# Attention row maxima from four part products in two row tiles, and the last four batches' layer-norm work moved from GpSimd to VectorE

## The chip, the cores and the metric

One core of a Trainium2 chip runs the whole program in one launch. The metric is the device time of that launch in microseconds, the median of several runs; lower is better. The core has five engines with a queue of instructions each: TensorE (PE in the profile, its weight loads PEld), VectorE (DVE), ScalarE (ACT), GpSimd (POOL) and SyncE (SP), which here only issues DMAs. Engines wait for each other through semaphores; a wait blocks everything that stands behind it on its engine.

## What is computed

Two layers of an adaptive-layer-norm network on 32 batches of 256 tokens with 128 features. The change lies in the first half of layer 0, attention with 16 heads of 8 features, followed by the second layer norm and the choice of two of eight experts for each token:

```
h   = layernorm(x) * (1 + scale_a[b]) + shift_a[b]
q,k = rope(h), rope(h @ w_k)              # 16 heads of 8 features, 256 tokens
p   = softmax(q @ k.T / sqrt(8))          # per head, 256 x 256
x   = x + gate_a[b] * ((p @ v) @ w_o + b_o)
h2  = layernorm(x) * (1 + scale_b[b]) + shift_b[b]
two of eight experts for each row of h2, by top-2 of h2 @ gate_w
```

A softmax does not change when a number is taken off all scores of a row, so the row maximum that the kernel subtracts has only to be near the true one.

## The kernel before

The program has stages: set-up, attention with the routing in front of the experts (the function `attention`), the experts of layer 0, and then layer 1, which is the longer part of the time. Only `attention` is touched.

**The loop.** Each engine has its own program, written out for every turn `i`; nothing but the written order and the semaphores decides what runs when. A turn handles several batches at different lags: batch `i` is normed, projected and roped; batch `i - 1` is stored and reloaded; `i - 2` (MAX) gets its row maxima; `i - 3` and `i - 4` their scores, exponentials and values; `i - 5` (OUT) the output projection; `i - 6` (LAST) the residual. Then come the second norm and the routing, for pairs of batches (`plan.groups`). There are 41 turns (0 to 40); `plan.var_at`, `root_at`, `norm_at`, `first_at`, `rank_at`, `quick_at` and `scattered_by` say in which turn a pair has its variance, root, modulation, choice, ranking and scatters. In the middle of the stage turns alternate: in even ones a pair is chosen (`top_of`, `first_of_top`, `first_chosen`, `second_chosen`), in odd ones it is ranked (`places`, `distances`, `slot_rows`, `limits`, `weights`).

**Three parts.** Each float32 of q and k is split into three bfloat16 parts. All nine products of parts are summed by one contraction over 9 x 8 = 72 rows (KROWS); `Q9` and `K9` hold these 72 rows, with two more for the row maximum, which the score product subtracts. SP stores the parts to DRAM (L512) and loads them back nine times over in eight DMAs for each batch (L525, L526, L528).

**Slots.** A turn on TensorE has eight slots (L1081): the maximum product of head 2p (L1012, two matmuls), four score matmuls (L1025), the maximum product of head 2p + 1, and values (L1039). Projections, transposes and logits stand between the slots. The scores of this batch's maximum are written to `MX`, a PSUM tile with two halves, head `h` to half `h % 2`. VectorE takes each head's maximum over the keys (`row_max`, L798) and so frees the half. The product of head h waits for the maximum of head h - 2. Between the maxima VectorE has its other steps: the bias (L921), the split of the maxima (L928, L930), rope (L955), the division by the sums (L977, L979), the statistics (L299) and the routing.

**The tail.** After the last maximum (turn 33) GpSimd does the residual (L609, L613), the variance (L554 to L560), the offset (L565), the modulation (L575, L581) and the scatters of rows to the experts' slots (L593), in this order on one queue. Each scatter is an indirect DMA of one tile of 128 rows; 128 are needed. When all places are known, SP writes eight blocks of padding rows (L541). Only then does the next stage start.

## Time and profile before

| | us |
|---|---|
| median of 3 runs | 3188.53 |
| lowest, highest | 3188.18, 3190.11 |
| profiled execution | 3185.01 |
| its span, first to last instruction | 3183.2 |

The profile's first part gives the busy time of each engine over the span: PE 2733.4 us (86%), DVE 2515.7 (79%), ACT 2236.9 (70%), POOL 2259.3 (71%). Its second part divides the span into 40 slices; the attention stage is in the first nine. The mean granted TensorE clock is 0.934 of full speed (2.4 GHz), and 0.5 stands for 1.2 GHz. The costliest group of this stage is the row maximum L798, 337.5 us in 512 instructions.

### The profile page before, as it was taken

The page shows a single profiled execution, that of the slowest core. Times are in us where ns is not written, and L with a number is a line of the kernel's source. Part 1 is how long each engine was busy: PE and PEld are TensorE (multiplying, and loading weights), DVE is VectorE, ACT ScalarE, POOL GpSimd, SP SyncE. Part 2 cuts the span into 40 slices and gives each one's busy share as a digit, 9 for nine tenths or more (in the row PEclk, how much of TensorE's full clock was granted, in tenths as well). Part 3 has the DMA queues.
Part 4 walks back from the last instruction along what each step waited for, and adds up shares of the span by engine and source line. Part 5 has one row for each costly group of instructions (what it writes and reads, how often), then busy time and mean ns, then how long its engine had stood idle before and what let it go on. Part 6 is the DMA issues. An engine that isn't in the chain of part 4 may idle for free. (4 is left out here: it accounts for less than half of the span.)

```text
span 3183.2 us, 56565 instructions
## 1 busy us (share of the span) xinstructions
PE 2733.4 (86%) x18747; PEld 2079.7 (65%) x18747; DVE 2515.7 (79%) x3550; ACT 2236.9 (70%) x4091; POOL 2259.3 (71%) x1731
## 2 busy tenths in 40 slices
PE   5999999829999977888888989888998888779984
PEld 3555555418999834666666666666766666679983
DVE  5788888723444446999999999999999999967993
ACT  2677777612222249999999999999999998656651
POOL 3356667552333348999999999999999999733664
PEclk6999999959999988999999999999999999889995
DMA  6555656316666662222222222222222222322231
GB/s 140 106 107 117 117 113 119 78 47 194 197 190 195 164 218 81 81 75 71 85 80 82 82 74 79 81 81 84 75 72 86 80 82 80 93 56 82 74 87 39
DMA packets 209174, 321.85 MB, mean 101 GB/s; under 512 B 37786, under 2 KB 118070, under 8 KB 204282
## 3 DMA queue, kind: packets, MB, share of 16 engines
q1 hardware_dynamic: 195666, 299.13, 34.9%
q0 software_dynamic: 12224, 18.42, 1.9%
q8 instruction: 161, 2.64, 0.4%
q14 instruction: 115, 0.94, 0.1%
q10 hardware_dynamic: 1008, 0.72, 0.1%
HBM read 269.92 MB, written 55.84 MB: 102 GB/s over the span
## 5 line engine op out<-in xcount | busy, mean ns | idle before, releaser
L1824 POOL TENSOR_TENSOR resid_x<-s_ux,s_B_rows 128x1024 f32<-128x1024 f32 x256 | 605.3, 2365 | 83.7 <-PE s_y L2554 82.7
L2385 DVE TENSOR_TENSOR_SCAN resid_x<-s_dA,resid_x 128x1024 f32<-128x1024 f32 x256 | 582.3, 2275 | 28.8 <-ACT s_dA L2036 23.2
L2393 DVE TENSOR_TENSOR_SCAN resid_x<-s_late,s_back_in 128x1024 f32<-128x1024 f32 x256 | 583.9, 2281 | 20.2 <-ACT s_late L2046 17.1
L2554 PE MATMUL s_y<-identity,resid_x 128*128 128x128 f32 x4096 | 558.7, 282 | 9.6 <-issue 8.8
L2554 PEld LDWEIGHTS s_y<-identity,resid_x 128*128 128x128 f32 x4096 | 498.6, 146 | 65.1 <-issue 40.6
L1832 POOL TENSOR_TENSOR resid_x<-resid_x,s_C_rows 128x1024 f32<-128x1024 f32 x192 | 454.0, 2365 | 0.9 <-DVE resid_x L2385 0.9
L798 DVE TENSOR_REDUCE a_row_max<-a_maxscores 128x2 f32<-128x512 f32 x512 | 337.5, 683 | 67.9 <-PE a_maxscores L1012 62.3
L2400 DVE TENSOR_TENSOR resid_x<-resid_x,s_C 128x1024 f32<-128x1024 f32 x320 | 382.7, 1196 | 6.0 <-PE s_C L2529 6.0
L2541 PE MATMUL s_back_in<-identity,resid_x 128*128 128x128 f32 x2048 | 292.3, 289 | 98.9 <-ACT resid_x L2057 52.6
L2036 ACT ACTIVATE s_dA<-s_dt,s_A 128x510 f32<-128x510 f32 x512 | 330.0, 676 | 66.2 <-DVE resid_x L2385 65.1
L2046 ACT ACTIVATE s_late<-s_dt,s_A 128x510 f32<-128x510 f32 x512 | 338.0, 710 | 0.0
L2541 PEld LDWEIGHTS s_back_in<-identity,resid_x 128*128 128x128 f32 x2048 | 239.8, 148 | 141.6 <-issue 81.9
L1324 POOL DMA_INDIRECT choice_outputs<-e_y,e_idx x142 | 137.8, 970 | 272.8 <-DVE e_y L1315 248.9
L668 ACT ACTIVATE a_probs<-a_scores 128x1024 f32<-128x1024 f32 x256 | 261.4, 1024 | 98.7 <-PE a_scores L1025 88.8
L1296 DVE TENSOR_TENSOR e_g<-e_silu,e_ps 128x512 f32<-128x512 f32 x142 | 97.7, 688 | 253.1 <-PE e_ps L1266 233.3
L1285 ACT ACTIVATE e_silu<-e_ps 128x512 f32<-128x512 f32 x142 | 84.8, 597 | 242.1 <-PE e_ps L1262 238.7
L3112 PE MATMUL k_psY<-k_coef_T,k_basis 128*128 128x128 f32 x2048 | 235.6, 277 | 7.1 <-ACT k_basis L3075 4.3
L3112 PEld LDWEIGHTS k_psY<-k_coef_T,k_basis 128*128 128x128 f32 x2048 | 232.9, 194 | 7.9 <-DVE k_basis L3003 4.7
L1012 PE MATMUL a_maxscores<-a_K,a_Q 72*128 72x256 bf16 x1024 | 203.9, 283 | 29.7 <-DVE a_row_max L798 17.1
L2581 PE MATMUL s_prep<-s_xT,k_coef_T 128*128 128x512 f32 x464 | 210.9, 596 | 2.7 <-ACT s_xT L2134 1.6
L2529 PE MATMUL s_C<-s_bc_parts,s_w_sel 96*128 96x512 bf16 x320 | 126.7, 396 | 87.1 <-DVE resid_x L2400 87.1
L2057 ACT ACTIVATE resid_x<-s_uT,s_bT 128x256 f32<-128x256 f32 x432 | 185.2, 498 | 0.8
(461 smaller groups left out, 5696.3 us busy)
## 6 DMA issues: line engine op xcount, KB each, us to landing
s_B_rows<-forward_rows SPq DMA_DIRECT2D x256, 256.0 KB, 3.3
e_w<-L_ffn_w_by_expert SPq DMA_DIRECT2D x71, 768.0 KB, 4.5
s_C_rows<-forward_rows SPq DMA_DIRECT2D x192, 256.0 KB, 3.3
a_Q<-split_qk SPq DMA_DIRECT2D x96, 192.0 KB
split_qk<-a_parts SPq DMA_DIRECT2D x32, 384.0 KB
e_x<-slot_inputs SPq DMA_DIRECT2D x71, 132.0 KB
a_K<-split_qk SPq DMA_DIRECT2D x64, 128.0 KB
s_late<-choice_outputs SPq DMA_DIRECT2D x16, 512.0 KB, 5.0
```

The source lines that it names most:

```text
L668: nc.scalar.activation(PT[:, q % 4].rearrange("p a b t -> p (a b t)"), ST[:, q % 2].rearrange("p a b t -> p (a b t)"), ACT.Exp, scale=SCAL ...
L798: nc.vector.tensor_reduce(mx[b % 2][:, h, :], MX[:, h % 2], AX.X, ALU.max).then_inc(S["max_done"], 1)
L1824: tt(R[s, 0], ux[par][:], brow[s % BRING][:].unsqueeze(1).broadcast_to([P, C2, W]), ALU.mult).then_inc(S["in_ready"], 1)
L1832: tt(r, r, crow[k % CRING][:].unsqueeze(1).broadcast_to([P, C2, W]), ALU.mult).then_inc(S["part_pool"], 1)
L2036: last = func(dA[:, c2, :, 1:T], dt[par][:, 0, c2, :].rearrange("p (g t) -> p g t", t=T)[:, :, 1:T], ACT.Exp, scale=Wt["A"][:, 0, c2, s:s ...
L2046: last = func(dec[s % 2][:, c2, :, 0:T - 1], dt[par][:, 1, c2, :].rearrange("p (g t) -> p g t", t=T)[:, :, 0:T - 1], ACT.Exp, scale=Wt["A" ...
L2385: nc.vector.tensor_tensor_scan(r, a, r, 0.0, ALU.mult, ALU.add).then_inc(S["scanned"], 1)
L2393: nc.vector.tensor_tensor_scan(r[:, ::-1], a[:, ::-1], b[:, ::-1], 0.0, ALU.mult, ALU.add).then_inc(S["scanned"], 1)
L2400: tt(r, r, CP[:].unsqueeze(1).broadcast_to([P, C2, W]), ALU.mult).then_inc(S["part_dve"], 1)
L2541: last = nc.tensor.transpose(bP[:, c2, k // TC, (k % TC) * P:(k % TC + 1) * P], bt[s % 2][:, k, c2 * P:(c2 + 1) * P], core.ident[:])
L2554: last = mm(YP[:, t, c2 * P:(c2 + 1) * P], R[s, d][:, c2, t * P:(t + 1) * P], core.ident[:], is_transpose=True, start=((s, d) == (0, 1) an ...
L3112: last = mm(psY[:, j % 2, k * D:(k + 1) * D], basis[j % 2][:, m, k * P:(k + 1) * P], WT[:, m, :], start=(m == EARLY[0] and k == 0), stop=( ...
```

## The change

Two parts, and a third that follows from the second.

- **Row maxima.** The product for the maximum no longer contracts all 72 rows, but 32 (`LEAD`): the four products of the first two parts. The order of the nine blocks in `Q9` and `K9` becomes different for heads 0 to 7 and for heads 8 to 15 (`Q_RUNS`, `K_RUNS`), so that these four stand in rows 0 to 31 for the first eight heads and in rows 32 to 63 for the last eight. A slot takes heads p and p + 8 together, one into each half of `MX`, with one semaphore step for the pair, and waits for both maxima of the pair before. The score product still contracts all 72 rows and the two of the maximum, so only the number that is subtracted changes a little. The reload takes 22 DMAs for each batch, each for eight heads.
- **The last four batches** (28 to 31). VectorE does their residual, variance, offset and modulation, in its own order.
- **Scatters** from turn 34 on are asked for as soon as their group is ranked, in eights.

```
+LEAD = 4 * DH
+Q_RUNS = (((0, 0, 2), (2, 0, 2), (4, 0, 3), (7, 2, 1), (8, 2, 1)), ((0, 0, 3), (3, 2, 1), (4, 0, 2), (6, 0, 3)))
+K_RUNS = (((0, 0, 2), (2, 1, 1), (3, 0, 1), (4, 2, 1), (5, 2, 1), (6, 0, 3)), ((0, 2, 1), (1, 2, 1), (2, 0, 2), (4, 0, 2), (6, 1, 1), (7, 0, 1), (8, 2, 1)))
...
-            sent = min(open_rows, sent + (4 if i <= B else 6)) if i < B + last else open_rows
+            sent = min(open_rows, sent + (4 if i <= B else 6)) if i < B + 2 else open_rows
...
-    LOADS = 3 * PARTS - 1
+    LOADS = sum(len(runs) for runs in (*Q_RUNS, *K_RUNS))
...
+    OWN_TAIL = B - 4
...
+                        for tile, w, runs in ((Q9[n], 0, Q_RUNS), (K9[n], 1, K_RUNS)):
+                            for half in range(2):
+                                for block, part, count in runs[half]:
+                                    sp.dma_start(tile[block * DH:(block + count) * DH, half * PAIRS:(half + 1) * PAIRS, :].rearrange("p h t -> p (h t)"),
+                                                 rows[w, part * DH:(part + count) * DH, half * PAIRS * T:(half + 1) * PAIRS * T]).then_inc(loaded[n], 16)
...
                 def row_max(i, h):
                     if live(i, MAX):
                         b = i - MAX
-                        dve.wait_ge(S["max_ps"], H * b + h + 1)
+                        dve.wait_ge(S["max_ps"], PAIRS * b + h // 2 + 1)
                         if h == 0:
                             at(dve, S["maxT_ps"], b - 1)
-                        nc.vector.tensor_reduce(mx[b % 2][:, h, :], MX[:, h % 2], AX.X, ALU.max).then_inc(S["max_done"], 1)
+                        nc.vector.tensor_reduce(mx[b % 2][:, h // 2 + PAIRS * (h % 2), :], MX[:, h % 2], AX.X, ALU.max).then_inc(S["max_done"], 1)
...
+                        if b >= OWN_TAIL:
+                            x_add(dve, nc.vector, b)
+                            new_stats(b)
+                    if i in plan.var_at and 2 * plan.var_at[i] >= OWN_TAIL:
+                        variance(dve, nc.vector, chain, plan.var_at[i])
+                    if i in plan.root_at and 2 * plan.root_at[i] >= OWN_TAIL:
+                        offset(dve, nc.vector, plan.root_at[i])
+                    if plan.early(i) is not None and plan.early(i) >= OWN_TAIL:
+                        modulate(dve, nc.vector, plan.early(i))
+                        modulate(dve, nc.vector, plan.late(i))
...
-                def max_scores(i, h):
+                def max_scores(i, p):
...
-                        at(pe, S["max_done"], H * b + h - 1)
+                        at(pe, S["max_done"], H * b + 2 * p)
                         for k in range(TC):
-                            last = mm(MX[:, h % 2, k, :], Q9[n][0:KROWS, h, k * P:(k + 1) * P], K9[n][0:KROWS, h, :], start=True, stop=True)
+                            for half in range(2):
+                                lead, h = slice(half * LEAD, (half + 1) * LEAD), p + PAIRS * half
+                                last = mm(MX[:, half, k, :], Q9[n][lead, h, k * P:(k + 1) * P], K9[n][lead, h, :], start=True, stop=True)
                         last.then_inc(S["max_ps"], 1)
...
                 def slot(i, p):
-                    max_scores(i, 2 * p)
+                    max_scores(i, p)
                     scores(i, p)
-                    max_scores(i, 2 * p + 1)
                     values(i, p)
```

Where it stands in the order: TensorE, two slots in the middle of the stage, before the change (`a_maxscores` is `MX`, `a_K` and `a_Q` the loaded parts, `a_out` the weighted values).

```order
L1124 MATMUL a_proj<-a_qk,a_rot 128x512
L1012 MATMUL a_maxscores<-a_K_0,a_Q_0 128x256 x2
L1025 MATMUL a_scores<-a_Q_2,a_K_2 128x256 x4
L1012 MATMUL a_maxscores<-a_K_0,a_Q_0 128x256 x2
L1039 MATMUL a_out<-a_probs,a_V 32x256 x4
L1012 MATMUL a_maxscores<-a_K_0,a_Q_0 128x256 x2
L1025 MATMUL a_scores<-a_Q_3,a_K_3 128x256 x4
```

The same place after the change.

```order
L1138 MATMUL a_proj<-a_qk,a_rot 128x512
L1027 MATMUL a_maxscores<-a_K_0,a_Q_0 128x256 x4
L1040 MATMUL a_scores<-a_Q_2,a_K_2 128x256 x4
L1054 MATMUL a_out<-a_probs,a_V 32x256 x4
L1027 MATMUL a_maxscores<-a_K_0,a_Q_0 128x256 x4
L1040 MATMUL a_scores<-a_Q_3,a_K_3 128x256 x4
```

The second pair of matmuls of a slot has moved in front of the scores; the number of matmuls is the same.

GpSimd at the end of the stage, from the last but one variance on, before the change (`slot_inputs` is what the scatters write, `neg_mean_rstd` the offset).

```order
L593 DMA slot_inputs<-a_choice_rows,a_slots 69376x132 x6
L609 TENSOR_TENSOR a_y<-a_y,a_gate_rows 128x256
L613 TENSOR_TENSOR resid_x<-resid_x,a_y 128x256
L554 TENSOR_TENSOR ln_dmean<-bn_stats 128x4
...
L593 DMA slot_inputs<-a_choice_rows,a_slots 69376x132 x6
L565 TENSOR_TENSOR neg_mean_rstd<-ln_mean,rstd 128x4
L575 TENSOR_TENSOR a_choice_rows<-a_choice_rows,a_mod_rows_b 128x2x128
```

And after it, the last steps of GpSimd in this stage.

```order
L523 TENSOR_TENSOR a_choice_rows<-a_choice_rows,a_mod_rows_b 128x2x128
L605 DMA slot_inputs<-a_choice_rows,a_slots 69376x132 x40
L536 UNCONDITIONAL_BRANCH
```

All that stood between the last scatters is gone from this queue. The offset and the modulations of the last pair now stand on VectorE, right behind the weights of the pair before:

```order
L891 RECIPROCAL a_choice_rows<-a_sum 128x2x4
L507 TENSOR_TENSOR neg_mean_rstd<-ln_mean,rstd 128x4
L517 TENSOR_TENSOR a_choice_rows<-a_choice_rows,a_mod_rows_b 128x2x128
L521 COPY a_choice_rows<-a_second_rows 128x4
L523 TENSOR_TENSOR a_choice_rows<-a_choice_rows,a_mod_rows_b 128x2x128
```

On VectorE these are new rows; nothing that stood there has gone.

## Rows read from the trace of the kernel before

**Rows 1.** Windows: us; busy us (instructions) by engine; granted clock, DMA share, GB/s.

```profile
100.00:500.00 400.00, 387.52 (x3541) 228.89 (x3539) 336.79 (x773) 296.57 (x497) 246.60 (x326) 1.00 0.58 114
...
616.00:716.00 100.00, 40.18 (x249) 20.68 (x248) 28.76 (x139) 23.25 (x46) 56.56 (x80) 0.56 0.15 45
```

**Rows 2.** The line L1100: times it runs, ns min/median/max, first and last start.

```profile
L1100 PE MATMUL a_proj<-identity,a_row_max x32: 269/270/417, 66.2 to 616.1; 128*32 128x128 f32 x32
```

**Rows 3.** Timeline, TensorE, one slot: start, us, engine, line, out<-in, count.

```profile
315.50 0.38 PE L1012 MATMUL a_maxscores<-a_K,a_Q 72*128 72x256 bf16 x2
...
315.62 0.42 PEld L1025 LDWEIGHTS a_scores<-a_Q,a_K 74*128 74x128 bf16 x4
...
315.73 0.60 PE L1025 MATMUL a_scores<-a_Q,a_K 74*128 74x256 bf16 x4
...
316.16 0.38 PE L1012 MATMUL a_maxscores<-a_K,a_Q 72*128 72x256 bf16 x2
...
316.48 0.64 PE L1039 MATMUL a_out<-a_probs,a_V 128*32 128x256 f32 x8
...
317.05 0.70 PE L1116 MATMUL a_proj<-a_qk,a_w_k 128*128 128x256 f32 x2
...
318.02 0.38 PE L1012 MATMUL a_maxscores<-a_K,a_Q 72*128 72x256 bf16 x2
```

**Rows 4.** Groups and waits, 100 to 500 us: count, busy, mean ns, idle before.

```profile
L798 DVE TENSOR_REDUCE a_row_max<-a_maxscores 128x2 f32<-128x512 f32 x363 | 239.6, 683 | 39.6 <-PE a_maxscores L1012 36.5 <-issue 0.7
L955 DVE TENSOR_TENSOR a_qk_sin<-a_proj,a_sin 128x512 f32<-128x512 f32 x22 | 15.0, 681 | 0.0
...
L979 DVE TENSOR_TENSOR a_out_rows<-a_proj,a_rden 128x256 f32<-128x256 f32 x22 | 9.3, 424 | 0.8
L921 DVE TENSOR_TENSOR a_y<-a_proj,a_bias_out 128x256 f32<-128x256 f32 x22 | 9.3, 422 | 7.7 <-PE a_proj L1156 7.7
...
L928 DVE CAST a_max_hi<-a_proj 32x128 bf16<-32x128 f32 x23 | 6.4, 279 | 5.3 <-issue 3.5 <-PE a_proj L1100 1.5
...
PEld a_maxscores L1012 <- DVE a_row_max L798: 38.6, 94, 1.3
```

**Rows 5.** Timeline, both directions of the handover between TensorE and VectorE.

```profile
305.82 0.69 DVE L798 TENSOR_REDUCE a_row_max<-a_maxscores 128x2 f32<-128x512 f32 x1
...
306.56 0.39 PE L1012 MATMUL a_maxscores<-a_K,a_Q 72*128 72x256 bf16 x2 [0.28 <-DVE a_row_max L798]
...
327.08 0.38 PE L1012 MATMUL a_maxscores<-a_K,a_Q 72*128 72x256 bf16 x2
...
327.50 1.35 DVE L798 TENSOR_REDUCE a_row_max<-a_maxscores 128x2 f32<-128x512 f32 x2 [0.24 <-PE a_maxscores L1012]
```

**Rows 6.** Timeline, VectorE's weights beside GpSimd's rope step, a ranking turn.

```profile
319.03 1.26 POOL L624 TENSOR_TENSOR a_qk_cos<-a_qk,a_cos 128x512 f32<-128x512 f32 x1 [2.28 <-ACT a_qk L720]
...
319.46 0.92 DVE L886 SCALAR_TENSOR_TENSOR a_spot<-a_limit,a_expd 128x64 f32<-128x64 f32 x1
```

**Rows 7.** Timeline, SP's first and last of eight loads; the first turn's wait.

```profile
315.71 0.55 SPq L525 DMA_DIRECT2D a_Q<-split_qk  x1
...
318.53 0.31 SPq L528 DMA_DIRECT2D a_K<-split_qk  x1
...
PEld a_maxscores L1012 <- DMA a_K<-split_qk: 11.8, 1, 11.8
```

**Rows 8.** Timeline, the tail: VectorE's weights, GpSimd's offset and last scatter.

```profile
675.01 0.20 DVE L888 RECIPROCAL a_choice_rows<-a_sum 128x8 f32<-128x8 f32 x1
...
679.93 0.22 POOL L565 TENSOR_TENSOR neg_mean_rstd<-ln_mean,rstd 128x4 f32<-128x4 f32 x1
...
692.77 0.21 DVE L888 RECIPROCAL a_choice_rows<-a_sum 128x8 f32<-128x8 f32 x1
...
704.63 0.98 POOL L593 DMA_INDIRECT slot_inputs<-a_choice_rows,a_slots  x1 [0.30 <-issue]
...
710.72 1.42 SPq L541 DMA_DIRECT2D slot_inputs<-a_pad_rows  x2
```

105 lines of the change are left out of this document (49 added, 56 removed).

## The prediction

> **What bounds the kernel now.** I read the windows table first, for where time lies. The change touches the attention stage alone, the first 718 of 3183 us; from 100 to 500 us TensorE is busy 97% of the time at the full clock (1.00, 2.4 GHz), VectorE 84%, ScalarE 74% and GpSimd 62%; from 616 to 716 us all of them are under 60% and the granted clock is 0.56 [rows 1]. The spacing of the 32 transposes of L1100, one for each turn of the loop, gives the turn: (616.1 - 66.2) / 31 = 17.74 us [rows 2].
>
> Then one slot of a turn in time. L1012 at 315.50, L1025 at 315.73, L1012 again at 316.16, L1039 at 316.48, what comes next at 317.05 [rows 3]: two maximum products cost TensorE 0.22 us, four scores 0.44, two more maximum products 0.32 (0.22, and 0.10 because the values that follow use another array shape), the values 0.57. That is 1.55 us for each of 8 slots, 12.4 us; what stands between the slots (projections, transposes, logits; the longest from 317.05 to 318.02) is 4.4 us, read in the same way. So TensorE works 16.8 of the 17.7 us and is held up for 0.9. The busy share of 97% overstates nothing much here.
>
> Third, who holds it up: L1012 waits for the row maxima, 38.6 us in the weight-load queue over 400 us, and the row maxima wait for L1012, 36.5 us [rows 4]. TensorE and VectorE pass two PSUM halves back and forth, head by head, and today the two halves hide most of it. The price of one such handover is in two places: a reduce that starts at 305.82 and lasts 0.69 lets L1012 start at 306.56, 0.06 us later; L1012 started at 327.08 lets a waiting reduce start at 327.50, 0.42 later [rows 5]. Together 0.48 us.
>
> **The change, part by part.** *Products.* The count stays at 32 for each batch; each contracts 32 rows in place of 72, and heads p and p + 8 go through two row tiles into the two PSUM halves. If the tiles run side by side, a slot's four products take 0.22 us and not 0.44. But the shape now changes twice more often: between products and scores, too, and between a full-array step and the products. At the 0.10 of [rows 3] a slot is 0.22 + 0.10 + 0.44 + 0.10 + 0.57 = 1.43 us, 0.12 less, and seven of the eight gaps between slots cost 0.10 more: 16.8 - 8 x 0.12 + 0.7 = 16.5 us of TensorE work for each turn. Bounds: tiles that do not overlap at all give 0.21 more in each slot (18.2 us); no cost for the switches gives 15.0. I take 16.5, since the four column tiles of the values do run side by side: eight passes of 256 columns within 0.64 us, where two such steps on the whole array take 0.22 each.
>
> The Trainium skill (page "TensorEngine Tiling (Array Packing)", section Key Properties) says that changing the tiling mode drains TensorE. The 0.10 us in front of the values agrees with it; no row shows a switch to row tiles. By the same page's PSUM Bottleneck section, tiling speeds up TensorE but not what empties PSUM, a rule that speaks against this change; the next paragraph works that out from rows.
>
> *The handover.* This decides. Before, product h needs only that reduce h - 2 is done. Now a pair's four products write both halves, need both reduces of the pair before, and tell VectorE once. While they run, VectorE has no maximum to take: every slot has a full handover of 0.48 us, hidden only where VectorE has other work after an odd head. A slot of VectorE is then 0.42 + 0.60 + 0.68 + 0.06 = 1.76 us (two reduces of 683 ns start 0.60 apart [rows 4, 5]), plus whatever stands between the even and the odd head, plus lateness. That is more than TensorE's 1.43.
>
> I wrote the recursion down for both kernels, slot by slot: a product starts at the later of "TensorE is free" and "the reduce it needs + 0.06", a reduce at the later of "VectorE is free" and "its product + 0.42"; VectorE's other steps at their own durations [rows 4]: 0.68 for L955, 0.42 for L921 and L979, 0.28 each for L928 and L930, about 0.2 for each of the small steps of the routing (L888 [rows 8]). For the kernel before it gives 17.79 us for a turn that ranks and 17.66 for one that chooses, mean 17.7 against the measured 17.74. So I trust it for the kernel after. There the slots of a ranking turn are 2.23, 2.21, 2.50, 3.40, 2.36, 2.00, 2.18, 2.07 = 18.95 us, of a choosing turn 2.11, 2.04, 2.50, 2.49, 2.36, 2.53, 2.36, 2.19 = 18.58. Two of them to follow: slot 4 has L955 between its heads, 0.42 + 0.60 + 0.60 + 0.68 + 0.06 = 2.36 (before: 1.55 to 2.0). Slot 3 of a ranking turn has `weights` there, whose L886 takes 0.92 us since it ends only after GpSimd's L624 (319.03 + 1.26) and not before [rows 6]; then 0.45 of small steps, then the second reduce: 3.40 in place of 2.51, where the second half used to let TensorE go on.
>
> The pair of turns grows from 35.45 to 37.53 us, 1.04 for each turn. Turns 10 to 33 are 24: +25 us. In turns 5 to 9, without routing, the recursion gives 17.2 to 17.5 against 16.1 to 16.3: +5.5. In turns 2 to 4 the granted clock is mostly half and TensorE, not VectorE, is the slower one; I take 0, between -2 and +2. Sum: +30.
>
> *Loads.* 8 DMAs for each batch become 22 of the same bytes in runs half as long. SP issues one each 0.40 us (315.71 to 318.53 is seven steps) [rows 7]: 22 take 8.8 us, so that the last is issued near 324.5, and the batch is needed at 329.2 or later. Behind them on SP wait the loads of gate and modulation rows, needed in the next turn, and the next store at 328.76. Cost 0; if a landing takes over 4 us longer, it shows in every turn. In the first turn nothing covers it (11.8 us wait for DMA [rows 7]): 0 to +3, I take 0.
>
> *Tail.* VectorE takes residual, variance, offset and modulation of the last four batches. What matters is the last offset: its input, the step before it on VectorE, is ready at 675.2, but GpSimd reaches L565 at 679.93, behind its scatters [rows 8]: 4.7 us. The four modulations at GpSimd's 0.73 become VectorE's 0.42 or so: 0.7 on the path. So the last slots and weights come 5.4 us earlier. The scatters are also asked for in eights, not sixes; five groups of eight at 1.27 us. The last group starts at 693.0 - 5.4 = 687.6, after the group before it (675.2 + 10.2 = 685.4), and ends at 697.8, where now the last starts at 704.63 and ends at 705.6: 7.8 us. Then SP's last pad rows, issued until 712.14 and slow while GpSimd scatters, must follow; I take -7 (bounds -4 and -9). What hides the added steps on VectorE: it is busy for 28.8 of the 100 us there [rows 1], and without that cover they would cost some 3.5 us for each pair of batches.
>
> **Sum.** The profiled execution spans 3183.2 us, timed 3185.0; 3185.0 + 25 + 5.5 - 7 = 3208.5. The median is 3.5 above the profiled one: 3188.5 + 23.5 = 3212.
>
> **The rivals.** *Serial tiles.* Weight loads are 0.10 apart for each product of 128 columns, as long as the product of 256 [rows 3]; if row tiles do not load side by side, a pair of halves costs 0.43 and VectorE is told at 0.63. The recursion then gives 19.67 and 20.05, +2.1 for each turn, 24 x 2.1 + 5 x 2.4 - 7 = +55: 3244. Against it: the column tiles of the values.
>
> *The other side: the handover is hidden and TensorE's own work decides.* If VectorE keeps ahead of TensorE, as in slots 2 and 3 of a choosing turn, a turn falls to TensorE's 16.5 us plus 0.5 of waits: 17.0, -0.7 for each of 29, -20, and -7 in the tail: 3162. It decides from the point at which VectorE's slot is under TensorE's 1.43 plus what follows it; for it speaks that slots 0, 2, 3 and 7 are near that; against it slots 1, 4, 5 and 6. Row tiles that save more than I think do not help, since they do not bound.
> For that side too, a page has a number: the Trainium skill ("TensorE: Matmul & The Clock Gate", section "Measured speedup vs the span model") gives 3.07 times for four row tiles; no row of this case shows it.
>
> *In between.* L886 and L831 no longer meet GpSimd's steps (-0.5 for each turn): 3200. Or the maxima part brings nothing and nothing lost: 3188.5 - 7 = 3182 to 3190.
>
> **How the numbers follow.** The forecast with its bounds (3197 to 3232) 0.62; serial tiles (3232 to 3260) 0.15; about nothing 0.08; hidden handover 0.15. A measurement tells 0.2%, 6.4 us, from no change. Faster by more: 0.15 and a little of the nothing case, 0.16; within: 0.07; slower: 0.77. The range leaves the hidden handover and the far end of the serial case out: 3186 to 3250. The likeliest case's own range is 3197 to 3232.
>
> **What would show it.** L1100 in the new trace at 18.7 us spacing; no row maximum within 0.4 us of its products; waits of the row maxima on products near 100 us where 36.5 stood; TensorE's waits on the row maxima up, its busy share down to some 90% at a full clock. Second starts in a slot's four products about 4 to 20 ns apart if the tiles run side by side, 0.1 if not. GpSimd's last scatter near 697.8, counted from the same place relative to the last turn, that is 7.8 earlier than now. I am wrong if the spacing is 17.7 or less; then the recursion lacks something that lets products and reduces of one pair overlap.

## The result, and the profile after

The changed kernel takes 3262.23 us (median of 6 runs, 3239.33 to 3285.43), the kernel before 3188.36 us (6 runs, 3187.10 to 3203.16). The ratio is 1.021, with a 95% interval from 1.018 to 1.025: slower by 74 us, where 24 were forecast, and outside the range. The sign was right, the size was not.

The profiled execution took 3285.43 us, the slowest of the six. The page of the changed kernel, its busy times, its granted clock in 40 slices (82 us each), and the row maxima:

```profile
PE 2799.3 (85%) x18747; PEld 2032.1 (62%) x18747; DVE 2521.2 (77%) x3584; ACT 2241.7 (68%) x4091; POOL 2246.4 (68%) x1697
...
PEclk6588898975999999999999999999999999889996
...
L801 DVE TENSOR_REDUCE a_row_max<-a_maxscores 128x2 f32<-128x512 f32 x512 | 336.4, 684 | 142.6 <-PE a_maxscores L1027 127.5
```

The third row answers to the 337.5 us in 512 instructions of the kernel before: the same work, with twice the waiting for products (127.5 us for 62.3). The second row is the surprise. The attention stage fills the first ten slices here, and in eight of them the clock is under nine tenths of full speed; in the page of the kernel before that is so in two of nine, the first and the last. The windows view of the changed kernel shows both at once (window and its length, then busy us of PE, PEld, DVE, ACT, POOL, granted clock, DMA share, GB/s):

```profile
380.00:400.00 20.00, 18.28 (x172) 8.64 (x169) 16.00 (x36) 14.35 (x26) 11.96 (x19) 1.00 0.37 107
100.00:500.00 400.00, 370.75 (x2924) 163.75 (x2916) 272.97 (x622) 246.71 (x404) 196.81 (x259) 0.83 0.33 94
...
415.45:434.14 18.69, 16.80 (x162) 7.95 (x158) 15.26 (x37) 13.13 (x23) 10.52 (x18) 1.00 0.37 106
434.14:453.27 19.13, 16.92 (x163) 8.07 (x162) 15.34 (x37) 13.44 (x24) 14.49 (x17) 1.00 0.43 115
...
471.96:495.14 23.18, 22.15 (x163) 10.03 (x162) 15.47 (x37) 13.65 (x24) 16.24 (x19) 0.73 0.33 97
```

The last three windows are single turns, cut at the transposes of L1114 (L1100 before). Turn n means here the window that begins with the transpose for batch n - 2. In the kernel's own count that transpose stands behind the first slot of turn n + 1, so a window holds seven slots of one turn and the first slot of the next: the windows of 18.69 us are mostly a ranking turn, those of 19.13 us mostly a choosing turn. In [rows 1] the clock of 100 to 500 us was 1.00; here it is 0.83. Where it is full, turns take 18.69 and 19.13 us by turns; where it falls to 1.2 GHz for part of a turn, 22 to 27 us. The whole of the difference between the two profiled executions, 100.4 us, divides like this. "Full-clock length" is what the same turn takes, in this trace or in that of `maxima_alone` below, where the clock is full in all of it:

| part of the stage | us |
|---|---|
| before the first transpose of L1114 (66.2 to 69.3) | +3.1 |
| turns 4 to 31, full-clock length against before | +26.5 |
| turns 4 to 31, what they took above that | +63.1 |
| turns 2 and 3, and 32 (half clock in most of them) | +14.4 |
| last transpose to the first expert matmul (102.0 to 95.8) | -6.2 |
| everything after it | -0.6 |

Of the 63.1 us some 2 are not the clock's: in turn 31 VectorE and ScalarE are both idle until 689.1, at the full clock, and TensorE waits 2.08 us for them; the trace does not show what held them. The other 61 go with the half-clock stretches. Of the 14.4 us, turn 2 has 2.2, turn 3 has 4.7 and turn 32 has 7.4.

### The profile page after: what moved, and what is told of

The parts are those of the page before. It is cut to its first block and busy times, and to the rows that moved or that the text cites. A ratio compares the mean times of both kernels' runs of the same rounds, so it can differ in the third digit from the quotient of the medians.

```text
span 3283.6 us, 57015 instructions
## 1 busy us (share of the span) xinstructions
PE 2799.3 (85%) x18747; PEld 2032.1 (62%) x18747; DVE 2521.2 (77%) x3584; ACT 2241.7 (68%) x4091; POOL 2246.4 (68%) x1697
## 5 line engine op out<-in xcount | busy, mean ns | idle before, releaser
L2407 DVE TENSOR_TENSOR_SCAN resid_x<-s_late,s_back_in 128x1024 f32<-128x1024 f32 x256 | 583.4, 2279 | 20.3 <-ACT s_late L2060 16.4
L801 DVE TENSOR_REDUCE a_row_max<-a_maxscores 128x2 f32<-128x512 f32 x512 | 336.4, 684 | 142.6 <-PE a_maxscores L1027 127.5
L1054 PE MATMUL a_out<-a_probs,a_V 128*32 128x256 f32 x2048 | 196.4, 461 | 4.0 <-ACT a_probs L671 2.8
L1040 PE MATMUL a_scores<-a_Q,a_K 74*128 74x256 bf16 x1024 | 186.0, 313 | 0.0
```

The lines of the kernel that those rows point to most:

```text
L801: nc.vector.tensor_reduce(mx[b % 2][:, h // 2 + PAIRS * (h % 2), :], MX[:, h % 2], AX.X, ALU.max).then_inc(S["max_done"], 1)
L2407: nc.vector.tensor_tensor_scan(r[:, ::-1], a[:, ::-1], b[:, ::-1], 0.0, ALU.mult, ALU.add).then_inc(S["scanned"], 1)
```

## Why the turn is longer at the full clock

TensorE in the changed kernel, two slots of a full-clock turn (start, us, engine, line, operation, count; in brackets the idle time before it and who ended it), then VectorE in the same place:

```profile
441.37 0.39 PE L1027 MATMUL a_maxscores<-a_K,a_Q 32*128 32x256 bf16 x4
441.69 0.61 PE L1040 MATMUL a_scores<-a_Q,a_K 74*128 74x256 bf16 x4
442.23 0.64 PE L1054 MATMUL a_out<-a_probs,a_V 128*32 128x256 f32 x8
443.75 0.39 PE L1027 MATMUL a_maxscores<-a_K,a_Q 32*128 32x256 bf16 x4 [0.88 <-DVE a_row_max L801]
```

```profile
441.81 0.69 DVE L801 TENSOR_REDUCE a_row_max<-a_maxscores 128x2 f32<-128x512 f32 x1 [0.81 <-PE a_maxscores L1027]
442.41 0.68 DVE L968 TENSOR_TENSOR a_qk_sin<-a_proj,a_sin 128x512 f32<-128x512 f32 x1
443.01 0.68 DVE L801 TENSOR_REDUCE a_row_max<-a_maxscores 128x2 f32<-128x512 f32 x1
```

Four products and the step into the scores take 441.69 - 441.37 = 0.32 us, which is 0.22 + 0.10: the tiles run side by side, at the cost that was forecast. (Single records put the starts of a slot's four matmuls at 441.372, 441.375, 441.492 and 441.494: pairs 2 to 3 ns apart.) Then the chain of the forecast follows step by step: 0.44 us to the first reduce, 0.60, L968 in between with 0.60, 0.68, and 0.06 to the next product. That is 2.38 us; 2.36 was forecast. The measured slots of a choosing turn, from 432.24 on, are 2.10, 2.03, 2.51, 2.49, 2.38, 2.60, 2.37, 2.51 (forecast 2.11, 2.04, 2.50, 2.49, 2.36, 2.53, 2.36, 2.19), of a ranking one 2.23, 2.20, 2.51, 3.13, 2.38, 2.02, 2.17, 2.18 (forecast 2.23, 2.21, 2.50, 3.40, 2.36, 2.00, 2.18, 2.07). Added up, the choosing turn takes 18.99 us (forecast 18.58) and the ranking one 18.82 (18.95). The kernel before, counted in the same way from 384.07 over 401.84 to 419.85, takes 18.01 and 17.77, where the recursion gave 17.66 and 17.79. So at the full clock the recursion was 0.4 us short for a choosing turn in both kernels, and what the change adds to a turn, 0.98 and 1.05 us, came out near the 0.92 and 1.16 of the forecast in part because that error cancels.

## The experiments

The experiments ran on three chips, between which the kernel before differs (medians 3178.0, 3194.6 and 3184.7 us), so each kernel is compared with runs of before on its own chip. Every run also gives its mean granted clock. As there are two levels only, half-clock time = 2 x (1 - mean clock) x span. Within each kernel the time follows it: over the 17, 19 and 7 runs of the kernel before, and the 6 of the changed one, by 0.31, 0.33, 0.37 and 0.36 us for each us at half clock, and what is left scatters by 2 to 3 us. So I split each difference: 0.35 x the added half-clock time is put down to the clock, the rest to the order of work. That is an estimate: over the 12 runs of `tail_alone` the slope is 0.24, over the 5 of `rows32_by_head` 0.43, so the last column is uncertain by about a tenth of the added half-clock time. For the changed kernel the two profiled executions are compared, since no other run of before on its chip has its clock here; with the mean of its six runs (3261.5 us, 555 us at half clock) the last column would be +30.

| kernel | runs | ratio to before, 95% | half-clock us, mean (before) | difference of means | at equal clock |
|---|---|---|---|---|---|
| changed | 6 | 1.021 (1.018 to 1.025) | 616 (423), profiled | +100 | +33 |
| maxima_alone | 4 | 1.021 (1.013 to 1.030) | 532 (438) | +68 | +35 |
| tail_alone | 12 | 0.999 (0.997 to 1.001) | 426 (423) | -2.8 | -4 |
| rows72_by_pair | 4 | 1.022 (1.018 to 1.027) | 491 (423) | +66 | +42 |
| rows32_by_head | 3 of 5 | 1.020 (1.015 to 1.024) | 497 (423) | +65 | +39 |
| rows32_only | 4 | 1.019 (1.014 to 1.023) | 491 (444) | +60 | +44 |
| rows64_only | 4 | 1.013 (1.008 to 1.017) | 433 (444) | +37 | +41 |
| filled | 4 | 1.029 (1.025 to 1.033) | 513 (423) | +93 | +62 |
| paired_reduce | 4 | 1.040 (1.033 to 1.046) | 708 (438) | +123 | +29 |
| half_keys | 10 | 0.993 (0.990 to 0.997) | 419 (438) | -20 | -13 |
| half_keys_before | 10 | 0.993 (0.990 to 0.996) | 422 (438) | -25 | -19 |

(For `rows32_by_head` the row takes the three quickest runs of five; the other two took 3284 and 3288 us, with 584 and 605 us at half clock.)

### The two parts apart

Tail alone: the changed kernel with the products, the loads and the order of the slots of before.

```
-                        dve.wait_ge(S["max_ps"], PAIRS * b + h // 2 + 1)
+                        dve.wait_ge(S["max_ps"], H * b + h + 1)
...
-                    max_scores(i, p)
+                    max_scores(i, 2 * p)
                     scores(i, p)
+                    max_scores(i, 2 * p + 1)
                     values(i, p)
```

> The change without its maxima part: 72-row products, head by head, the eight loads and the order of the kernel before; only the steps of the last four batches on VectorE and the scatters in eights are kept. My theory has the tail as an own gain of 7 us: about 3181 us (3178 to 3185), turns of 17.62 and 18.16 us as before, full granted clock from 100 to 600 us, last scatter about 7.8 us earlier than before. Rival: the tail only moves work, SP's last pad rows end when they ended before: 3187 to 3190. If the lost clock of the changed kernel had come from this part, it would show here as half-clock stretches between 100 and 600 us.

Measured: no difference, 0.999 (0.997 to 1.001), though the interval holds the forecast 0.998 too. Its trace says why the time does not show the gain:

```profile
403.62:421.77 18.15, 17.49 (x162) 10.12 (x162) 15.30 (x37) 13.27 (x22) 14.48 (x17) 1.00 0.59 123
440.52:471.23 30.71, 30.71 (x163) 16.36 (x163) 16.77 (x37) 13.75 (x22) 15.30 (x19) 0.51 0.35 72
...
633.10:718.80 85.70, 36.86 (x250) 19.68 (x249) 36.33 (x171) 22.90 (x46) 42.95 (x46) 0.59 0.19 55
```

From the last transpose to the first expert matmul it is 85.7 us, where the kernel before has 102.0. But one turn at 440.52, alike in work to the one at 403.62, took 12.6 us more at half clock, with TensorE busy in all of it. The tail part cannot have caused that: up to the kernel's own turn 33 this program issues the instructions of the kernel before, in the same order. To see whether it comes back, and what the kernel before does on another chip, two single runs:

> The tail part alone once more, for a second trace. If the half-clock stretch of 44 us at 441 us was chance, it is gone or stands elsewhere, and without one the time is 3181 - 17 = 3164 us. If it comes from the change, it stands at the same place, and 3178 to 3183 us follow.

> The kernel before, word for word, for a trace from the chip on which the experiments run (its runs there lie between 3164 and 3193 us). If its turns are 17.4 to 18.2 us with the full granted clock from 100 to 600 us, the tail (last transpose of the row maxima to the first expert matmul) is 102 us, and the time is 3176 to 3190, then the tail part's 16 us are real and were hidden in the run of the tail alone by its one half-clock stretch. If the tail is under 95 us here, the tail part gains less than its trace suggests.

They took 3185.53 and 3185.36 us. The stretch at 441 us was gone; another began at 596 us. The kernel before had none between 93 and 629 us and a tail of 100.2 us; the tail part's second one was 94.1 us, in half clock nearly from its start. Counted from the start of the last offset (679.93 in [rows 8]), a stretch at half clock in all of them, the next stage's first matmul is 38.2 and 36.5 us away in two traces of before, and 32.9, 32.8 and 33.1 us in the changed kernel and the two of the tail part: some 4 us of the gain are in every trace. The rest (2 to 12 us) depends on the clock in turns 31 to 34.

The maxima part alone, on the kernel before:

```
...
-                    max_scores(i, 2 * p)
+                    max_scores(i, p)
                     scores(i, p)
-                    max_scores(i, 2 * p + 1)
                     values(i, p)
```

> The kernel before with the maxima part alone (four part products, row tiles, pairs, 22 loads), its tail as before. It should be slower than the changed kernel by what the tail part brings, 4 to 8 us, so 3265 to 3270 on the chip where the changed kernel took 3262; relative to the kernel before 1.022 to 1.026. If the tail part brings nothing when the maxima are changed, it is the changed kernel's 1.021. Turns at full clock 18.69 and 19.12 us.

Measured: 3253.24 us against 3184.72, 1.021, as the changed kernel. Its full-clock turns are the changed kernel's, 17.35 us in turns 5 and 6 (16.41 before), then 18.69 and 19.1:

```profile
136.68:154.03 17.35, 16.07 (x153) 7.29 (x150) 12.78 (x25) 12.18 (x19) 6.30 (x7) 1.00 0.53 143
245.10:264.19 19.09, 16.93 (x163) 8.08 (x162) 15.30 (x37) 13.39 (x24) 12.01 (x14) 1.00 0.41 109
264.19:282.88 18.69, 16.79 (x161) 7.95 (x158) 15.26 (x37) 13.15 (x23) 10.52 (x18) 1.00 0.46 104
```

So the whole loss is the maxima part's. By time the tail part cannot be told from nothing here either.

### Is the handover what costs, at the full clock?

Half of the reduce: VectorE takes the maximum over the first 128 of the 256 keys; the other half of each row is left out of the maximum (the number taken off is then another one). Once on the changed kernel, once on the kernel before.

```
-                        nc.vector.tensor_reduce(mx[b % 2][:, h // 2 + PAIRS * (h % 2), :], MX[:, h % 2], AX.X, ALU.max).then_inc(S["max_done"], 1)
+                        nc.vector.tensor_reduce(mx[b % 2][:, h // 2 + PAIRS * (h % 2), :], MX[:, h % 2, :, 0:P], AX.X, ALU.max).then_inc(S["max_done"], 1)
```

> The changed kernel with VectorE's maximum taken over the first 128 of the 256 keys only (half of the elements; the number taken off the scores is then another one). A row maximum costs about 0.42 us instead of 0.68. Theory of the handover: the slot's chain falls from 1.76 to 0.42 + 0.34 + 0.42 + 0.06 = 1.24 us, under TensorE's 1.43; turns fall from 18.7 and 19.1 us to 16.6 to 17.3, TensorE's own work. Rival (TensorE's own work is what takes 18.7): turns above 18.3. Half-clock time should be under that of the changed kernel (555 us in the mean of its runs) if waits matter, the same if only rows matter. Time 3185 to 3210, or by the rival above 3250.

> The same edit on the kernel before. There VectorE's maxima are nearly hidden: turns fall only from 17.74 to TensorE's 16.8 us or so, in turns 5 to 7 not at all from 16.4. Time 29 x 0.8 = 25 us under the kernel before. If the two kernels with the short maxima are within 10 us of each other at equal granted clock, the row tiles buy and cost TensorE nothing, and the whole of the change's loss at full clock is the handover.

Measured: the changed kernel falls from 2.1% above before to 0.7% under it. Windows of two turns each, of the changed kernel with half the keys, then of the kernel before with half the keys:

```profile
436.57:454.33 17.76, 16.85 (x162) 8.09 (x162) 11.83 (x37) 13.37 (x24) 14.18 (x17) 1.00 0.44 122
454.33:471.82 17.49, 16.67 (x162) 7.96 (x159) 11.09 (x37) 13.15 (x23) 10.73 (x18) 1.00 0.44 115
```

```profile
424.30:441.53 17.23, 16.87 (x163) 10.52 (x162) 12.24 (x37) 13.16 (x22) 13.96 (x17) 1.00 0.65 126
441.53:458.30 16.77, 16.75 (x162) 10.41 (x159) 11.22 (x37) 13.22 (x24) 11.04 (x18) 1.00 0.60 120
```

The reduce went from 684 to 416 ns, and nothing on TensorE was touched, yet the changed kernel's turn fell by 1.2 and 1.4 us. That is the handover theory's doing; the rival, TensorE's own work, asked for turns above 18.3. The forecast of 16.6 to 17.3 us was still a little low, since 0.8 to 0.9 us of waits remain: one choosing step, L840, now takes up to 0.93 us beside a step of GpSimd (0.18 at 445.17 in the changed kernel). At equal clock the two kernels stand 6 us apart (-13 and -19), inside the 10 that were named, but their two traces, with the same half-clock time, are 13 us apart (3155.6 and 3142.6), and the tail part stands in one of them alone. The turns say which part of that is TensorE's: its busy time is the same (16.85 and 16.67 us against 16.87 and 16.75), and the 0.5 to 0.7 us by which the changed kernel's turns are still longer are waits. So the row tiles neither gain nor cost TensorE anything that shows, and with half of the keys the handover is mostly, not wholly, hidden. And the half-clock time fell to that of before, although these products contract 32 rows: 385 to 444 us in ten runs, where `maxima_alone`, on the same chip and with the same products, has 478 to 582 in four. That comes back below.

One step for both heads: the pair's two reduces become one, and the other steps of VectorE come behind it, beside the handover.

```
-                    if live(i, MAX):
+                    if live(i, MAX) and h % 2 == 0:
...
+                        nc.vector.tensor_reduce(mx[b % 2][:].rearrange("p (u q) k -> p q u k", u=2)[:, h // 2], MX[:], AX.X, ALU.max).then_inc(S["max_done"], 2)
```

> The changed kernel with one edit on VectorE: the maxima of a pair's two heads are taken by one step over both PSUM halves (128x1024), right when the pair's products are done, and what stood between an even and an odd head now comes behind the pair, beside the handover. Nothing else moves. Theory of the handover: the slot's chain is 0.42 + about 1.24 + 0.06 = 1.72 us, but VectorE's other steps no longer stand in it up to 0.48 us for each slot; the recursion with this order gives 17.3 to 17.8 us for a turn at the full clock, against 18.69 and 19.12, and TensorE's waits fall by half. Time without the clock's part 3262 - 29 x 1.3 = 3224, and less half-clock time: 3190 to 3225. Rival (the longer turn is TensorE's own work, its changes of array shape): turns stay at 18.5 or more and the time within 10 us of the changed kernel's 3262.

Measured: 3308.22 us, the slowest of all; forecast 3190 to 3225. The first turns went as expected (17.10 us in turn 6 at the full clock, against 17.35), the choosing turns did not:

```profile
147.26:164.36 17.10, 16.06 (x153) 7.29 (x149) 12.30 (x17) 12.07 (x19) 7.29 (x13) 1.00 0.42 117
...
513.42:533.65 20.23, 16.99 (x162) 8.08 (x162) 16.65 (x29) 13.50 (x24) 14.74 (x18) 1.00 0.40 109
533.65:562.72 29.07, 29.07 (x161) 11.79 (x159) 14.22 (x30) 13.85 (x24) 13.66 (x21) 0.50 0.25 72
```

The second row is a choosing turn at the full clock, 20.23 us long. Its timeline, GpSimd and VectorE:

```profile
523.00 1.28 POOL L634 TENSOR_TENSOR a_roped<-a_qk_cos,a_qk_sin 128x512 f32<-128x512 f32 x1 [0.46 <-DVE a_qk_sin L968]
523.04 1.28 DVE L834 TENSOR_TENSOR a_is_max<-a_biased,a_top 128x32 f32<-128x32 f32 x1
...
528.29 1.16 POOL L642 TENSOR_TENSOR a_parts<-a_left,a_parts 128x512 bf16<-128x512 f32 x1 [2.06 <-ACT a_parts L750]
528.39 1.10 DVE L846 TENSOR_TENSOR a_choice<-a_cand,a_choice_rows 128x32 f32<-128x32 f32 x1
```

L834 takes 0.19 us at 529.97 in the same turn, and L846 0.18 us at 447.53 in the changed kernel. Here they take 1.28 and 1.10 us, and end when GpSimd's step does, the collision of L886 with L624 in [rows 6] again, in new places. There it cost 0.7 us in every second turn; here it costs 2 us in the other ones, all ahead of the next pair's reduce. Moving VectorE's small steps into the shadow of the handover moved them onto GpSimd's long ones. Then the clock did the rest: 708 us at half clock. That the pair's step as such saves what it should is seen in turns 5 and 6 alone.

### Where the clock goes

Two theories: TensorE's waits in every slot, or the products' few rows. Each of the two was taken back by itself. By head: 32 rows, row tiles and loads as changed, but one head at a time in the order of before.

```
...
+                        at(pe, S["max_done"], H * b + h - 1)
+                        half = h % 2
+                        lead, head = slice(half * LEAD, (half + 1) * LEAD), h // 2 + PAIRS * half
+                        for k in range(TC):
+                            last = mm(MX[:, half, k, :], Q9[n][lead, head, k * P:(k + 1) * P], K9[n][lead, head, :], start=True, stop=True)
+                        last.then_inc(S["max_ps"], 1)
```

> The changed kernel with the pair taken apart: still 32 rows for each product, the same row tiles, layout and 22 loads, but head p before the scores and head p + 8 behind them, each with a semaphore step of its own and waiting only for the maximum two heads back, as before. No two row tiles run side by side. Theory one (the handover of a pair makes TensorE idle in every slot, and that idleness takes the granted clock down): TensorE has hardly a wait on the row maxima, the clock stays full from 100 to 600 us, a turn is 16.8 + 8 x 0.3 for the switches, about 19.2 us, and the time is 3188 + 29 x 1.5 - 7 = 3225. Theory two (products that use 32 of 128 rows load the array too little, whatever the waits): half-clock stretches of 20 us as in the changed kernel, 160 us of them in 100 to 650 us, and 3250 or more.

Measured: 3251.11 us. TensorE is busy in all of a turn, and the full-clock turns are 18.99 and 19.14 us, near the 19.2 expected. But the clock was half from 23 to 194 us, and from 86.58 on TensorE was busy all the time (three windows of a turn each, then two at full clock):

```profile
86.58:115.92 29.34, 29.34 (x144) 9.55 (x140) 12.16 (x19) 12.31 (x17) 4.83 (x4) 0.50 0.19 58
115.92:148.07 32.15, 32.15 (x154) 11.47 (x150) 13.28 (x22) 12.69 (x18) 6.28 (x6) 0.50 0.23 52
148.07:180.22 32.15, 32.15 (x153) 11.47 (x149) 13.67 (x24) 12.70 (x18) 6.28 (x6) 0.50 0.28 81
245.60:264.74 19.14, 19.14 (x163) 8.90 (x162) 15.43 (x37) 13.29 (x22) 7.27 (x9) 1.00 0.39 95
264.74:283.73 18.99, 18.99 (x162) 8.76 (x158) 15.64 (x38) 13.52 (x24) 9.68 (x16) 1.00 0.35 96
```

In this trace waits cannot explain the half clock. It is a trace of one of the two slowest runs, though: the three quickest have 472 to 513 us at half clock, which is still above all 17 runs of before (392 to 466). By pair: all 72 rows, no row tiles, the loads of before, but the pair's handover.

```
...
+                        at(pe, S["max_done"], H * b + 2 * p)
+                        for half in range(2):
+                            h = p + PAIRS * half
+                            for k in range(TC):
+                                last = mm(MX[:, half, k, :], Q9[n][0:KROWS, h, k * P:(k + 1) * P], K9[n][0:KROWS, h, :], start=True, stop=True)
+                            last.then_inc(S["max_ps"], 1)
```

> The changed kernel with all 72 rows contracted again, no row tiles, the eight loads of before, but with the pair's handover: the products of heads p and p + 8 in a row ahead of the scores, both waiting for both maxima of the pair before (each tells VectorE by itself). Its rows are the full ones, its waits those of the changed kernel less 0.2 us for each slot. Theory one (idleness by the handover): turns at full clock of 18.6 to 19.1 us, half-clock stretches again, perhaps fewer: 3225 to 3260. Theory two (too few rows): the same turns, but the clock stays full: 3188 + 30 - 7 = 3211. If the handover were not what costs the 1.2 us for each turn at full clock, the turns would be at 17.7 and the time at 3181.

Measured: 3243.10 us; full-clock turns of 18.93 and 19.32 us, the handover's cost once more without any row tile. The clock is up by 99 us, as before, but falls three times between 200 and 510 us, for 75 us in all:

```profile
285.90:305.22 19.32, 17.52 (x162) 10.37 (x162) 15.41 (x37) 13.38 (x24) 14.52 (x17) 1.00 0.56 114
470.49:495.51 25.02, 23.40 (x162) 13.16 (x159) 15.45 (x37) 13.84 (x24) 13.90 (x21) 0.72 0.44 84
```

So few rows alone, and waits alone, both cost clock. To have the rows without anything else, the kernel before with one number changed, to 32 and to 64 rows:

```
-... Q9[n][0:KROWS, h, k * P:(k + 1) * P], K9[n][0:KROWS, h, :] ...
+... Q9[n][0:4 * DH, h, k * P:(k + 1) * P], K9[n][0:4 * DH, h, :] ...
```

> The kernel before with one edit: the maximum products contract the first 32 of the 72 rows (four other part products than the change takes, q0k0, q1k1, q2k2, q0k1); order, waits, loads and the tail as before. Theory of the rows (fewer rows load the array less and the granted clock follows): half clock from the start until near 190 us though TensorE is busy nearly all the time, short half-clock stretches later; time 3178 + 70 = 3250. Theory of idleness (only waits cost the clock): the clock is as before. Both: if a step into a product of 32 rows costs 0.10 us as the step into the values does, 16 more such steps each way make turns of about 19.0 us, so 3178 + 29 x 1.3 = 3216 by the theory of idleness; if only row tiles side by side cost that, the turns stay at 17.4 to 18.2.

> The kernel before with its maximum products contracting the first 64 of the 72 rows, nothing else. Theory of the rows: 64 rows are near 72, so the clock comes up at 95 to 120 us and hardly falls. If the step into another array shape is what makes the turn longer, it depends on the shape and not on the work: 64 rows are a half array where 72 rows take the whole, so turns of about 19.0 us as with 32 rows, and 3178 + 38 = 3216. If nothing changes, 3178 us.

Measured: 3253.50 and 3226.25 us. The first 64 rows of the 72 leave one of the nine products of parts out of the maximum, the first 32 five. Both have the same turns at the full clock. A slot of the kernel with 64 rows:

```profile
300.02 0.39 PE L1012 MATMUL a_maxscores<-a_K,a_Q 64*128 64x256 bf16 x2
300.34 0.61 PE L1025 MATMUL a_scores<-a_Q,a_K 74*128 74x256 bf16 x4
300.88 0.39 PE L1012 MATMUL a_maxscores<-a_K,a_Q 64*128 64x256 bf16 x2
301.20 0.64 PE L1039 MATMUL a_out<-a_probs,a_V 128*32 128x256 f32 x8
301.77 0.44 PE L1109 MATMUL a_proj<-identity,a_xn 128*128 128x128 f32 x2
```

0.32, 0.54, 0.32, 0.57: against [rows 3] (0.22, 0.44, 0.32, 0.57) each step between a product of 32 or 64 rows and a full one costs 0.10 us, whatever the rows, 1.75 us for a slot in place of 1.55. The turns, 19.15 and 19.01 us here, 19.14 and 18.99 with 32 rows, follow from that alone, and so does nearly all of the +41 to +44 us at equal clock. The waits of TensorE's weight loads on the maxima between 100 and 500 us are 21.1 us in 70 places in both, while its matmuls fill 399.7 of the 400 us in both. What differs is the clock: half-clock times of 412, 425, 432 and 460 us with 64 rows (before: 413 to 473), of 466, 474, 502 and 521 with 32. With 32 rows the turns that drain the stage run at half clock; with 64, the last of them is at full:

```profile
655.74:683.36 27.62, 27.62 (x148) 10.17 (x144) 13.48 (x34) 10.65 (x16) 8.38 (x16) 0.50 0.12 23
```

```profile
642.23:659.24 17.01, 16.01 (x148) 7.18 (x145) 12.81 (x35) 9.85 (x14) 7.67 (x15) 1.00 0.15 38
```

These last two windows are the same turn, 32, of the kernel with 32 rows and of that with 64.

One thing that the theory of the rows foretold did not come: half clock until near 190 us. With 32 rows the clock is full from 103 us on, with 64 from 102, so the long first stretch of `rows32_by_head` is not what 32 rows do by themselves. Turns 3 and 4 of `rows32_only`:

```profile
88.69:112.02 23.33, 23.14 (x143) 8.61 (x139) 11.75 (x19) 11.62 (x17) 4.84 (x4) 0.69 0.34 64
112.02:130.35 18.33, 18.33 (x153) 8.12 (x149) 12.86 (x23) 12.25 (x19) 5.90 (x6) 1.00 0.51 103
```

And the two traces differ by 107 us at half clock (520 and 413), of which 31 lie behind 900 us, where the two programs are alike. So the reading on the rows rests on four runs against four, which do not overlap but stand only 6 us apart.

Last, the changed kernel with more work in it: two of the four score products of a slot are written twice.

```
-                            for k in range(TC):
+                            for k in (0, 0, 1):
                                 last = mm(ST ...
```

> The changed kernel with work added: of each slot's four score products two are written twice, with the same result to the same place, 0.22 us more of TensorE in each slot, less than what TensorE waits there (0.3 to 0.9 us in most slots). Theory one: TensorE's waits shrink, half-clock stretches between 160 and 650 us are gone or fewer, and the kernel with more work is faster: turns stay at 18.7 to 19.3 us and the time is 3212 to 3235, against 3262. Theory two, or idleness being no cause: as many half-clock stretches as in the changed kernel, 3262 or more.

Measured: 3274.66 us, no gain. The clock did what was expected (full from 100 to 435 us; 31 us at half clock between 100 and 650 us where the changed kernel has 161), but the turns did not:

```profile
245.77:265.73 19.96, 18.61 (x178) 9.64 (x178) 15.52 (x37) 13.49 (x24) 11.96 (x15) 1.00 0.42 105
265.73:285.28 19.55, 18.44 (x177) 9.51 (x174) 15.26 (x37) 13.13 (x23) 10.54 (x17) 1.00 0.34 100
```

The 0.22 us for each slot fit into the waits only in part: half of the added 1.76 us, 0.85, is in the turn, since in the slots with a projection behind them TensorE is not the one that waits. What the clock gave was paid for in work, and the stage's last turns were at half clock again: over whole runs half-clock time is 482 to 531 us, hardly less than the changed kernel's 485 to 617.

So in this kernel each of the two costs clock: waits, firmly (72 rows: 491 us by pair against 423 by head; and 532 us in `maxima_alone`, 555 in the changed kernel, fall to 419 when only the reduce is shortened), and rows, by a smaller sample (32 against 64 at equal waits: 491 against 433). That the two add up to the changed kernel's 485 to 617 us is an inference. TensorE's own idle time on the row maxima, from 100 to 500 us, puts the kernels in the order of the first cause: 9.6 us in the kernel before and 14.0 in half_keys, which have the full clock there, and 27.7 in the changed kernel, 29.2 in rows72_by_pair, 34.8 in maxima_alone, which have not. What is not settled is how rows and waits act together: half_keys has 32 rows and some waits and loses nothing, rows32_only has no idle time that shows and loses some. Whether two row tiles side by side cost clock beyond their rows and the pair's waits was not tried by itself. When a single stretch at half clock begins is chance at this level of detail, as the two traces of the tail part show.

The Trainium skill ("TensorE: Matmul & The Clock Gate", section "A second HAM failure mode: psum-queue depth-cycling") describes a kernel whose TensorE idles for very short times while it cycles through PSUM, and whose clock goes up and down for that. The trace agrees with it: the longest wait of TensorE's weight loads on the maxima between 100 and 500 us is 1.4 us, and the clock falls all the same. What is said here of rows rests on the runs alone.

## Why the prediction was wrong, step by step

- **The bound and the handover price** (0.42 and 0.06): right. They came out of the trace of before and met the slots of the changed kernel.
- **The recursion**: right at the full clock in what the change adds. 18.58 and 18.95 us were forecast for a choosing and a ranking turn, 18.99 and 18.82 measured; turns 10 to 30 grew by 21.6 us or 1.03 each, where 1.04 stood; turns 5 to 9 by 4.8 for 5.5. The forecast counted 24 turns of the first kind, and there are 21: turn 31 takes 16.66 us at the full clock in `maxima_alone`, 16.77 before. The check that gave the recursion its trust, 17.7 against 17.74 us, was in part luck: 17.74 is the mean over all 31 spacings, with turns of 16.4 us and turns at half clock in it, while the turns that were modelled take 17.62 and 18.16, 17.9 in the mean.
- **Row tiles side by side, 0.10 us for each change of shape**: right, both. The serial-tiles rival, 3244 and nearest to the measured time, is refuted all the same.
- **The clock**: the step that failed. The sum has no term for it. The text said "TensorE's waits on the row maxima up, its busy share down to some 90% at a full clock": the waits and the busy share came (18.28 of 20 us from 380 to 400), the full clock did not. What the runs showed in its place is 61 us in turns 4 to 31 of the profiled execution, and some 12 more in turns 3 and 32: the changed kernel stayed at half clock until 155 us, but for 3.4 us, where the kernel before came up at 95. [Rows 1] held the warning: 0.56 in the tail, where TensorE pauses.
- **The first turns**: "I take 0, between -2 and +2", since at half clock TensorE is the slower one, failed too, if by less. Where scores and values do not yet stand between the products, TensorE waits for the row maxima at half clock as well: from 60 to 90 us 10.9 us in 9 places, where the kernel before has 3.2 us in 6 from 60 to 86. Turn 2 of both kernels, at half clock in both, the changed one first; then one of the waits:

```profile
69.27:89.91 20.64, 15.55 (x78) 5.66 (x76) 12.66 (x21) 7.52 (x12) 4.84 (x4) 0.50 0.29 81
```

```profile
66.15:84.56 18.41, 17.85 (x77) 8.60 (x76) 12.31 (x21) 7.39 (x12) 4.84 (x4) 0.50 0.50 108
```

```profile
80.89 0.60 PE L1027 MATMUL a_maxscores<-a_K,a_Q 32*128 32x256 bf16 x4 [1.98 <-DVE a_row_max L801]
```

- **Loads**: 22 for 8 cost nothing that shows in a turn. The first turn's wait for them is 9.7 us (11.8 in [rows 7]), and the first product starts at 50.48 us, where it started at 51.10. So the 3.1 us by which the first transpose is later are not the loads': between that product and the transpose TensorE waits 8.4 us for row maxima, 3.2 us before (which was also at the full clock from 57 to 64 us).
- **Tail**: -7 forecast, -6.2 in the profiled executions, though partly by other ways. In the tail part alone the last scatter came 13.4 us earlier after the last transpose (88.6 to 75.2), not 7.8; in the changed kernel only 3.4 us, since its last turns were at half clock. By time it is 4 us, and 0 cannot be excluded.
- **The hidden-handover rival** (3162): refuted for this kernel, and its condition confirmed by half_keys: with VectorE's slot under TensorE's the time was 3167 us, where the kernel before has 3185 on that chip.
- **The range**: it allowed for errors of the terms in the sum, none for a term left out. At equal clock the change costs 30 to 33 us, so 3212 (+24, with the tail at -7) was near for the part that it covered. The three runs of before agreed within 2 us and showed nothing of how far this kernel's time moves with the clock; on the chips of the experiments its runs spread over 22 to 40 us.

## What to carry to other kernels

Before work of TensorE is made shorter or put behind a wait, ask what it does to the granted clock: here a handover that costs 1 us for each 18 us turn cost twice that again by half-clock stretches in the profiled, slowest execution (one and a half times by the mean of six), while shorter waits brought the clock back without any change on TensorE. The two row tiles here fill the two PSUM halves at once and so use up the double buffering that hid the handover, and the pair's handover costs as much without row tiles (rows72_by_pair); products that were not the bound gain nothing from them, and each switch to 32 or 64 rows and back costs 0.10 us. And give each run's mean clock beside its time: it took the scatter of this kernel from tens of microseconds to 3.

No kernel here that takes the maximum over all keys beats the kernel before. The tail part alone is the nearest, at 0.999 (0.997 to 1.001). half_keys_before is faster, but takes the maximum over half of the keys, and nothing here shows how near that comes to the true one for other scores; what it shows is that VectorE's time in the maxima is worth having also in the kernel before (16.8 and 17.2 us for a turn in place of 17.6 and 18.2).

## What the runs showed of the hardware that was not expected

- The granted clock can stay at 1.2 GHz while TensorE is busy without a pause: from 86.58 to 180.22 us in rows32_by_head (three turns, busy 93.64 of 93.64 us), and for a whole turn of 30.71 us in tail_alone, with 72 rows.
- Products of 32 and of 64 rows cost the same to switch to and from, 0.10 us each; products of 72 rows cost nothing beside the full array.
- The 22 shorter loads move the same bytes with less time of the DMA engines. From 100 to 600 us, the maxima part alone and then the kernel before with 32 rows and its 8 loads; the last two columns are DMA share and GB/s:

```profile
100.00:600.00 500.00, 452.76 (x3985) 209.06 (x3977) 376.19 (x870) 336.20 (x558) 279.30 (x372) 0.94 0.38 103
```

```profile
100.00:600.00 500.00, 499.70 (x4078) 228.25 (x4070) 392.09 (x887) 346.54 (x573) 287.66 (x383) 0.99 0.54 106
```

- A step of VectorE that meets a long step of GpSimd ends with it, not after its own 0.19 us: 1.28 and 1.10 us in paired_reduce. It depends on the step: the reduce at 524.41 kept its 1.23 us beside GpSimd's L639 in the same trace.
